# Delta scan on one core: each of a block's four VectorE operations over all rows of the state at once, in place of two halves

## The reference, cut to what matters

```python
def step(S, inp):
    qt, kt, vt, at, bt = inp
    Sk = jnp.einsum('bhde,bhe->bhd', S, kt)
    outer_Sk_k = Sk[..., :, None] * kt[..., None, :]
    outer_v_k = vt[..., :, None] * kt[..., None, :]
    S_new = at * S - at * bt * outer_Sk_k + bt * outer_v_k
    ot = jnp.einsum('bhd,bhde->bhe', qt, S_new)
    return (S_new, ot)
_, O = jax.lax.scan(step, S0, (q, k, v, a, bgate))
```

## Time and profile before

| | |
|---|---|
| median of 3 runs | 2109.55 us |
| lowest and highest | 2106.34 and 2110.17 us |
| the profiled execution's own time | 2114.28 us |
| its span in the profile | 2112.6 us |
| VectorE busy | 1586.0 us (75%), 3116 instructions |
| ScalarE busy | 917.4 us (43%), 2009 instructions |
| TensorE matmul busy | 1368.3 us (65%) |
| GpSimd busy | 226.5 us (11%) |

### The profile page before, as it was taken

One profiled execution on the slowest core, in us unless ns is written; L12 is line 12 of the kernel. 1 busy time (PEld: TensorE's weight loads), 2 busy tenths in 40 slices (PEclk: granted clock), 3 DMA queues, 4 the chain that ended last, 5 costly groups with the idle time before them and its releaser, 6 DMA issues. The chain is left out here.

```text
span 2112.6 us, 44670 instructions
## 1 busy us (share of the span) xinstructions
PE 1368.3 (65%) x15216; PEld 726.3 (34%) x15216; DVE 1586.0 (75%) x3116; ACT 917.4 (43%) x2009; POOL 226.5 (11%) x218
## 2 busy tenths in 40 slices
PE   4489999999899999970998560000000058840998
PEld 2115444444444444350665240000000023420665
DVE  5498888888788888243565664998999989972665
ACT  4407777777677777851343551001222200030343
POOL 6000000000000000015044000000000000016044
PEclk9859999999999999985999665555555579975999
DMA  3420111111111100031243239002211110011243
GB/s 101 119 67 24 32 28 28 29 28 28 29 29 36 42 6 3 2 101 49 54 66 51 80 107 198 36 0 50 60 47 44 35 45 0 0 40 53 52 68 45
DMA packets 125839, 101.05 MB, mean 48 GB/s; under 512 B 23666, under 2 KB 108211, under 8 KB 125235
## 3 DMA queue, kind: packets, MB, share of 16 engines
q1 hardware_dynamic: 108738, 84.79, 15.8%
q0 software_dynamic: 11264, 8.92, 2.9%
q10 hardware_dynamic: 5616, 4.47, 1.2%
HBM read 55.98 MB, written 31.21 MB: 41 GB/s over the span
## 5 line engine op out<-in xcount | busy, mean ns | idle before, releaser
L696 DVE TENSOR_REDUCE att_negmax<-att_ps_max 128x1 f32<-128x1024 f32 x512 | 614.1, 1221 | 112.0 <-PE att_ps_max L567 91.7
L684 ACT ACTIVATE att_probs<-att_ps_prob 128x512 f32<-128x512 f32 x1024 | 561.5, 598 | 244.3 <-PE att_ps_prob L582 232.9
L567 PE MATMUL att_ps_max<-av_k_op,av_q_op 81*32 81x512 bf16 x4096 | 417.1, 404 | 42.9 <-DMA av_q_op<-terms_q 18.9
L582 PE MATMUL att_ps_prob<-av_q_op,av_k_op 99*32 99x512 bf16 x4096 | 406.3, 385 | 9.3 <-ACT att_probs L684 1.2
L599 PE MATMUL att_ps_acc<-att_probs,att_vq 128*32 128x256 f32 x4096 | 308.2, 381 | 0.0
L1878 PE MATMUL out_ps_y<-all_bo_row,all_ones 1*128 1x128 f32 x2 | 0.8, 480 | 439.2 <-PEq L104 439.2
L567 PEld LDWEIGHTS att_ps_max<-av_k_op,av_q_op 81*32 81x32 bf16 x4096 | 108.7, 97 | 184.6 <-DVE att_negmax L696 80.4
L582 PEld LDWEIGHTS att_ps_prob<-av_q_op,av_k_op 99*32 99x32 bf16 x4096 | 108.0, 95 | 174.7 <-ACT att_probs L684 131.1
L599 PEld LDWEIGHTS att_ps_acc<-att_probs,att_vq 128*32 128x32 f32 x4096 | 125.7, 111 | 82.5 <-issue 5.9
L1878 PEld LDWEIGHTS out_ps_y<-all_bo_row,all_ones 1*128 1x128 f32 x2 | 0.5, 304 | 439.5 <-issue 439.5
L1145 ACT ACTIVATE moe_moe_gate<-moe_moe_ps_h 128x256 f32<-128x256 f32 x122 | 46.7, 383 | 213.9 <-PE moe_moe_ps_h L1086 213.9
(11 more groups left out here) (274 smaller groups left out, 2149.7 us busy)
## 6 DMA issues: line engine op xcount, KB each, us to landing
moe_moe_xin<-expert_rows SPq DMA_DIRECT2D x182, 72.0 KB, 1.9
av_k_op<-terms_k SPq DMA_DIRECT2D x48, 216.0 KB
av_q_op<-terms_q SPq DMA_DIRECT2D x144, 72.0 KB
solve_M_and_windows<-solve_X SPq DMA_DIRECT2D x16, 256.0 KB, 3.1
solve_M_and_windows<-solve_k SPq DMA_DIRECT2D x16, 256.0 KB, 3.7
terms_q<-qkv_parts_q SPq DMA_DIRECT2D x8, 384.0 KB, 2.6
terms_k<-qkv_parts_k SPq DMA_DIRECT2D x8, 384.0 KB, 3.2
all_w_all<-in_f_w SPq DMA_DIRECT2D x24, 128.0 KB, 2.5
```

Source lines behind the costliest of these rows:

```text
L567: mm = pe.matmul(ps_max[c * STRIP:(c + 1) * STRIP, a % 2, k * CH:(k + 1) * CH], q_op[s][0:R_ALL, h, at:at + STRIP], k_op[s][0:R_ALL, h, k ...
L582: mm = pe.matmul(ps_prob[c * STRIP:(c + 1) * STRIP, j % 2, :], k_op[s][0:R_END, h, at:at + STRIP], q_op[s][0:R_END, h, half * CH:(half + 1 ...
L684: act.activation(probs[:, j % PROBS, :], ps_prob[:, j % 2, :], ACT.Exp).then_inc(s_exp, 1)
L696: dve.tensor_reduce(negmax[:, s % 2, a:a + 1], ps_max[:, a % 2, :], AX.X, ALU.max, negate=True).then_inc(s_maxed, 1)
```

## The change

Each of the four operations is issued once a block, over all four rows. The two semaphores `s_step[0]` and `s_step[1]` become one, still with 4 counts a block. The loop over `halves` goes away, and so does the list. What is computed for each element, the windows, the buffers, ScalarE's operations and the DMAs stay.

```diff
-        s_step = m.sems("step", 2)
+        s_step = m.sem("step")
...
-                for r in range(2):
-                    sp.wait_ge(s_step[r], STEP * WB * (w + 1))
+                sp.wait_ge(s_step, STEP * WB * (w + 1))
...
-                        for r, rows in enumerate(halves):
-                            wait_used(dve, s_step[r], STEP * n)
-                            dve.tensor_tensor(p1[:, c % 2, rows, :, 0:D],
-                                              St[:, rows, :].unsqueeze(2).to_broadcast([P, R // 2, L, D]),
-                                              xw_t.unsqueeze(1).to_broadcast([P, R // 2, L, D]), ALU.mult
-                                              ).then_inc(s_step[r], 1)
+                        wait_used(dve, s_step, STEP * n)
+                        dve.tensor_tensor(p1[:, c % 2, :, :, 0:D],
+                                          St[:, :, :].unsqueeze(2).to_broadcast([P, R, L, D]),
+                                          xw_t.unsqueeze(1).to_broadcast([P, R, L, D]), ALU.mult
+                                          ).then_inc(s_step, 1)
                         dve.wait_ge(s_addend, n + 1)
-                        for r, rows in enumerate(halves):
-                            dve.wait_ge(s_step[r], STEP * n + 1)
-                            dve.tensor_reduce(xv[:, p, rows, tok], p1[:, c % 2, rows, :, :], AX.X, ALU.add
-                                              ).then_inc(s_step[r], 1)
-                        for r, rows in enumerate(halves):
-                            dve.wait_ge(s_step[r], STEP * n + 2)
-                            dve.tensor_tensor(p2[:, rows, :, 0:L],
-                                              xv[:, p, rows, tok].unsqueeze(2).to_broadcast([P, R // 2, D, L]),
-                                              kd_t.unsqueeze(1).to_broadcast([P, R // 2, D, L]), ALU.mult
-                                              ).then_inc(s_step[r], 1)
+                        dve.wait_ge(s_step, STEP * n + 1)
+                        dve.tensor_reduce(xv[:, p, :, tok], p1[:, c % 2, :, :, :], AX.X, ALU.add
+                                          ).then_inc(s_step, 1)
+                        dve.wait_ge(s_step, STEP * n + 2)
+                        dve.tensor_tensor(p2[:, :, :, 0:L],
+                                          xv[:, p, :, tok].unsqueeze(2).to_broadcast([P, R, D, L]),
+                                          kd_t.unsqueeze(1).to_broadcast([P, R, D, L]), ALU.mult
+                                          ).then_inc(s_step, 1)
                         dve.wait_ge(s_decayed, n + 1)
-                        for r, rows in enumerate(halves):
-                            dve.wait_ge(s_step[r], STEP * n + 3)
-                            dve.tensor_reduce(St[:, rows, :], p2[:, rows, :, :], AX.X, ALU.add
-                                              ).then_inc(s_step[r], 1)
+                        dve.wait_ge(s_step, STEP * n + 3)
+                        dve.tensor_reduce(St[:, :, :], p2[:, :, :, :], AX.X, ALU.add
+                                          ).then_inc(s_step, 1)
...
-                        wait_used(act, s_step[1], STEP * n)
+                        wait_used(act, s_step, STEP * n)
...
-                wait_used(act, s_step[1], STEP * (n - 2) + 2)
+                wait_used(act, s_step, STEP * (n - 2) + 2)
```

More of the change, by code:

```diff
@@ L1742, in body @@
             def body(i):
-                halves = [slice(r * R // 2, (r + 1) * R // 2) for r in range(2)]
                 for p in range(2):
```

## The result

The changed kernel takes 2138.82 us (median of 4 runs, 2136.11 to 2141.64) against 2108.36 us for the kernel before (4 runs, 2106.34 to 2110.17). The ratio is 1.0145, 95% interval 1.0127 to 1.0162: slower, by 30.5 us. The forecast was 2141 us and +31.7 us.

What follows compares the result with a forecast made beforehand. The prediction took VectorE's serial scan as the bound: 254 ns a block of overhead saved against 502 ns of overlap lost, 248 ns more over 128 blocks, +31.7 us on the 2109.55 us median, so 2141 us, range 2128 to 2150 us.

Steps and rivals of the forecast that it cites:

- The scan is the path, with no cover: VectorE's scan: its 239.2 us lie on the path in full, with no work beside them to take up a change.
- Overhead saved, 254 ns a block: Scan block: four instructions fewer save 2 x 67 + 2 x 60 = 254 ns, if all else stayed.
- A dependent operation starts its predecessor's duration plus 35 ns later: Scan: each whole operation needs the result just ahead, so it is priced as duration plus 35 ns; lost overlap 502 ns.
- The four durations: Scan's whole operations L1753, L1760, L1764, L1771: 588, 453, 424, 453 ns; with four gaps 2058 ns a block against 1810.
- The hop: L1753's strided reads: 82 ns more per 128 elements, taken per element (588 ns whole); per instruction 506 ns, total +21.2 us.
- That kind of wait costs no more.: Scan's loop: waits that compare with a register add nothing to the 35 ns gap, as in the convolution's loop.
- The loop's stall: Where VectorE's loop body starts over in the scan: two waits for its own issue, 5.5 us, kept in the sum.
- third rival: Scan's dependent waits: waits and register work between operations cost some 50 ns each, 0.2 us a block, +57 us; chance 0.05.
- the first rival: Scan's loop: the shorter body of 291 instructions no longer stalls, +26.2 us, about 2136 us; chance 0.15.
- The range: Whole kernel: +18.4 to +40.4 us, 2128 to 2150 us, leaving out the fast rival, dear wait and 0.1 for the rest.
- ScalarE and SyncE move nothing: Beside the scan: ScalarE's results are ready before needed, SyncE's stores and loads get a longer window; no change in time.
- The faster rival: Scan: overlap survives for dependent operations, 1.56 us a block, -32.5 us, about 2077 us; break-even 128 ns an instruction; chance 0.04.

Runs made afterwards that it cites:

- the independent whole operations: Changed kernel with each operation reading what its predecessor wrote one block ago, output not the reference's: 2075.02 us, ratio 0.9833 against the kernel before.
- the turned windows: ScalarE turns each window to token by element, so the first multiplication reads without a hop: kernel before 2089.53 us (0.9893), changed kernel 2119.82 us (1.0043).

## Why the prediction was right, and where only its sum was

- **The scan is the path, with no cover.** Right: the scan grew by 30.0 us, the median by 30.5.
- **Overhead saved, 254 ns a block.** Right: the independent whole operations take 1.555 us against 1.81.
- **A dependent operation starts its predecessor's duration plus 35 ns later.** Right in the loop: 2066 - 595 - 453 - 425 - 453 = 140 ns, four gaps of 35. Shown from both sides, by whole operations without the dependence and by halves with it.
- **The four durations.** Forecast 588, 453, 424 and 453 ns, measured 595, 453, 425 and 453. The hop is per element, which the turned windows confirm: 83 ns for 128 elements, 170 for 256. The row that the prediction quotes from the Trainium skill, "Vector Engine (DVE) Microarchitecture Reference", section "Measured stream behaviour on trn2", is for hops of 4 KiB. Here a hop is 512 bytes and costs 170 / 256 = 0.66 ns an element.
- **"That kind of wait costs no more."** This step failed for a quarter of the blocks. It took one gap for all, and asked whether waits on a register cost more. The cost came where the waits are on constants: the built program puts the step wait there in an instruction of its own. Two gaps of 105 ns in place of 35 make the 32 written-out blocks 4.5 us dearer than the sum had them. The halves had hidden it: 1.81 to 1.82 us in both parts, since the wait there is for a half that had already ended (L1753's first half ends at 1500.52, L1760 starts at 1500.72). Where the halves are put in dependent order it shows, 0.47 us against 0.40 in the written-out blocks. My third rival looked at the right place and had the wrong mechanism: it priced the waits and the register work in between, yet four fulfilled waits more at each place left the block at 2.06 us. What counts is which instruction holds the last-coming wait.
- **The loop's stall.** The sum kept it; the first rival, with 0.15, was what happened: the body of 291 instructions pays none. That took 5.5 us off. The term was wrong, and it nearly cancels the 4.5 us above: 31.7 + 4.5 - 5.5 = 30.7 us, against 30.5 measured. That the total came within 1.2 us of the forecast is in part luck.
- **The range.** Its lower end, +18.4 us, is the prediction's own sum with the hop per instruction and half of the stall gone, 21.2 - 2.75. From the lower bound by the minima, which the text names there, it would have been 24.1 - 10.5 - 2.75 = +10.9 us. And the chances of the forecast and its three rivals already add up to 1, so the 0.1 for the rest has no place. The result lies well inside either range.
- **ScalarE and SyncE move nothing.** Right for ScalarE, and nothing in the traces speaks against it for SyncE: ScalarE is idle 1.6 us ahead of L1781, as forecast (1.73 in the written-out blocks), and releases no operation of VectorE.
- **The faster rival** would have needed a price per instruction under 128 ns in the scan. It is (2066 - 1298) / 4 = 192 ns with the dependence and (1555 - 1298) / 4 = 64 without. The Trainium skill, "VectorE: DVE Perf Modes", section "Rules for kernel authors", with its advice to keep down the number of chained operations and not the semaphores, points the wrong way here: eight halves at 1.81 us beat four whole operations at 2.07.

Why a wait in an instruction ahead costs 70 to 90 ns more than one on the operation itself stays open. So does where between 323 and 419 instructions the stall sets in. Nor does any run tell what the 35 ns between dependent operations are made of, since every dependent pair here also has a semaphore between it.

## What to carry to other kernels

In a serial chain on one engine, count a dependent step as the whole duration plus the gap to the next (35 ns here), and an independent one by its start to start (some 65 ns beyond its elements here). Two halves that alternate can therefore beat one whole operation, although they are twice as many: at 128 against 256 elements they did, by 0.25 us a block. Whole operations won here only where each no longer needed the result of the one ahead. If an operation has two waits, look in the built program which one it carries, and let it be the one that comes last.

## What the runs showed that was not expected

- A last-coming wait in the instruction ahead of the operation costs 70 ns (a wait instruction, written-out blocks) or 90 ns (a register instruction, in the loop) more than on the operation itself.
- Where the loop's body starts over, VectorE stalls for 2.7 to 3.0 us with 419 or 427 instructions and not at all with up to 323. The Trainium skill, "Runtime: NRT & Kernel Launch", section "Instruction fetch mechanics", says that a taken branch stalls if its target is outside the two blocks of 256 instructions that are held. The trace agrees in that the longer bodies stall and the shorter don't, and gives the price; what is held, no run here shows.
- ScalarE takes 622 ns to turn 256 elements, where its plain copy of 32 elements takes 243 ns.
